# A convolution and attention kernel on one core: output stores issued before most of the loads of the image after next, and the orders inside attention written anew

## What is computed

```python
per_g = perception.reshape(b, M, 9 * C, h, w)              # 3x3 neighbourhood; M=32 groups of C=16
hdn = relu(einsum('bmchw,mdc->bmdhw', per_g, w1) + b1)     # 64 hidden channels a group
x1 = x + einsum('bmdhw,mcd->bmchw', hdn, w2) + b2
theta, phi, g = (projections of x1 from 512 to 128 channels)
attn = softmax(einsum('bno,bom->bnm', theta, phi), axis=-1)
y = einsum('bnm,bmo->bno', attn, g)
z = einsum('co,bno->bcn', w_w, y) + w_b                    # then batch norm with stored statistics
out = z + x1
```

## Time and profile before

| what | value |
|---|---|
| time, median of 3 runs (lowest to highest) | 1736.95 us (1734.25 to 1737.31) |
| the profiled execution, its own time | 1739.32 us |
| its span in the profile | 1737.5 us |
| mean granted TensorE clock | 0.962 of full speed |
| TensorE busy | 1551.6 us (89%) |
| VectorE, ScalarE, GpSimd busy | 875.1, 765.2 and 249.6 us |
| main memory traffic | 361.84 MB, 208 GB/s over the span; the DMA queue 64.2% busy |

### The profile page before, as it was taken

How to read it: one execution, slowest core, us unless ns; L and a number is a source line. 1 busy time by engine, 2 the same in 40 slices (tenths; PEclk the granted TensorE clock), 3 DMA queues, 4 the chain that set the end, 5 groups by cost and what they waited for, 6 DMA issues and landing times.

```text
span 1737.5 us, 23755 instructions
## 1 busy us (share of the span) xinstructions
PE 1551.6 (89%) x8324; PEld 838.4 (48%) x8324; DVE 875.1 (50%) x1200; ACT 765.2 (44%) x1205; POOL 249.6 (14%) x134
## 2 busy tenths in 40 slices
PE   5899898989989899898998989899898998989986
PEld 1265453645445364453645436354553654536455
DVE  0265363645627365373744627455273653737464
ACT  1444354444535454354443535454344543534442
POOL 0030020301103020020301203021030300203021
PEclk8899999999999999999999999999999999999998
DMA  9675766757576485765757566575765757656325
GB/s 284 156 240 186 242 216 190 245 185 245 180 232 232 152 272 175 242 229 151 260 192 246 187 218 227 175 259 179 250 230 148 257 187 238 216 183 233 124 92 175
DMA packets 179006, 361.84 MB, mean 208 GB/s; under 512 B 12336, under 2 KB 120880, under 8 KB 178992
## 3 DMA queue, kind: packets, MB, share of 16 engines
q1 hardware_dynamic: 178992, 361.66, 64.2%
HBM read 252.56 MB, written 109.05 MB: 208 GB/s over the span
## 4 chain that ended last, share of the span: by engine, by line
issue 85%; POOL 12%; DMA 1%; DVE 1%; PE 1%; POOLq 0%; ACT 0%; DVEq 0%; SPq 0%
POOL probs L885 12%; DMA rows_out<-probs 1%; DMA x_lo<-rows_out 1%; DVE x_lo L752 0%; PE ps L463 0%; PE ps L465 0%; PE ps L464 0%; DVE probs L743 0%; ACT x_hi L613 0%; POOLq L883 0%; DVE x L770 0%; POOLq L896 0%; DVE arena L758 0%; DVE neg_max L725 0%; ACT y_hi L623 0%
## 5 line engine op out<-in xcount | busy, mean ns | idle before, releaser
L397 PE MATMUL ps<-windows,w_main 128*64 128x512 f32 x2048 | 501.2, 616 | 51.9 <-ACT hidden L585 19.0
L885 POOL TENSOR_TENSOR probs<-probs,row_inv 128x1024 f32<-128x1024 f32 x128 | 248.9, 1950 | 1459.2 <-DVE row_inv L731 1459.2
L585 ACT ACTIVATE hidden<-ps,columns 128x512 f32<-128x512 f32 x512 | 315.4, 689 | 248.5 <-PE ps L408 228.6
L397 PEld LDWEIGHTS ps<-windows,w_main 128*64 128x64 f32 x2048 | 130.3, 138 | 375.8 <-issue 191.8
L417 PE MATMUL ps<-hidden,w2s 128*32 128x512 f32 x1024 | 148.9, 656 | 77.5 <-DVE x L706 77.5
L752 DVE TENSOR_TENSOR x_lo<-x_lo,x_hi 128x1024 fp32r<-128x1024 f32 x128 | 170.4, 1331 | 70.4 <-ACT x_hi L613 69.5
L713 DVE TENSOR_TENSOR x_lo<-x,x_hi 128x512 fp32r<-128x512 f32 x128 | 88.5, 691 | 221.8 <-ACT x_hi L593 219.9
L706 DVE SCALAR_TENSOR_TENSOR x<-ps,columns,windows 128x512 f32<-128x512 f32 x128 | 95.3, 744 | 200.4 <-DMA out<-x 104.6
L608 ACT ACTIVATE probs<-ps,neg_max 128x1024 f32<-128x1024 f32 x128 | 142.8, 1116 | 102.7 <-DVE neg_max L725 98.3
L613 ACT CAST x_hi<-x_lo 128x1024 fp32r<-128x1024 f32 x128 | 134.1, 1047 | 113.5 <-DMA x_lo<-rows_out 113.5
L725 DVE TENSOR_REDUCE neg_max<-ps 128x1 f32<-128x1024 f32 x128 | 155.2, 1213 | 53.6 <-PE ps L450 51.4
(11 more groups left out here) (55 smaller groups left out, 1541.8 us busy)
## 6 DMA issues: line engine op xcount, KB each, us to landing
windows<-in_x SPq DMA_DIRECT2D x208, 562.0 KB, 7.6
rows_out<-probs SPq DMA_DIRECT2D x128, 512.0 KB, 5.1
x_lo<-rows_out SPq DMA_DIRECT2D x128, 512.0 KB, 4.4
out<-x SPq DMA_DIRECT2D x64, 512.0 KB, 3.6
windows<-in_x SPq DMA_DIRECT2D x32, 421.5 KB, 7.1
windows<-in_x SPq DMA_DIRECT2D x32, 409.9 KB, 8.2
windows<-in_x SPq DMA_DIRECT2D x32, 281.0 KB, 9.3
rows_out<-hidden SPq DMA_DIRECT2D x16, 512.0 KB, 2.8
```

The source lines that it names most:

```text
L397: mm(ps[rows, hidden_bank(s, q), :], w_main[:, p, which, :], shifted(windows[:, w, :], unit // UNITS, half), start=True, stop=False, skip_ ...
L585: activation(hidden[:, q, :], ps[:, hidden_bank(s, q), :], ACT.Relu, bias=b1s[:, column:column + 1]).then_inc(hidden_ready, 1)
L885: nc.gpsimd.tensor_tensor(rows, rows, row_inv[:, e].to_broadcast([P, PIXELS]), ALU.mult).then_inc(normalized, 1)
```

## The change

No operation is added or taken away; only orders change, on SyncE, TensorE, ScalarE and VectorE. GpSimd's order stays. The core of the diff:

```diff
@@ SyncE, batch
-                    load_freed(n + 1, GROUPS - 1)
+                    load_freed(n + 1, 3)
+                send_g(n)
                 send_row(n, 0)
-                send_g(n)
+                fetch_g(n)
+                send_row(n, 1)
                 fetch_row(n, 0)
-                send_row(n, 1)
-                fetch_g(n)
+                send_row(n, 2)
                 fetch_row(n, 1)
...
                 store_quarter(n, 2)
                 if has_second:
                     load_freed(n + 2, 0)
-                    load_freed(n + 2, 1)
                 store_quarter(n, 3)
                 if has_second:
+                    load_freed(n + 2, 1)
                     load_freed(n + 2, 2)
@@ TensorE, batch
                 scores(n, 3)
+                if has_next:
+                    mains(n + 1, 0, range(0, 3))
                 scores(n, 4)
...
                 attend(n, 0, has_next)
-                if has_next:
+                scores(n, 7)
+                output(n, 0, 0)
+                if has_next:
+                    mains(n + 1, 1, range(1, 3))
                     dx(n + 1, 0)
-                    mains(n + 1, 1, range(1, 3))
-                outputs(n, 0)
-                scores(n, 7)
+                output(n, 0, 1)
...
-                    image_slot(n + 1, 4)
-                    mains(n + 1, 5, every)
+                    mains(n + 1, 4, range(0, 4))
+                attend(n, 3, has_next)
+                if has_next:
+                    dx(n + 1, 3)
+                    hidden_shared(n + 1, 4)
+                output(n, 3, 0)
+                output(n, 3, 1)
+                if has_next:
+                    mains(n + 1, 5, range(0, 4))
                     hidden_shared(n + 1, 5)
-                attend(n, 3, has_next)
-                if has_next:
                     dx(n + 1, 4)
-                outputs(n, 3)
-                if has_next:
-                    image_slot(n + 1, 6)
-                    image_slot(n + 1, 7)
+                    mains(n + 1, 6, range(0, 4))
+                    hidden_shared(n + 1, 6)
+                    dx(n + 1, 5)
+                    mains(n + 1, 7, range(0, 4))
+                    dx(n + 1, 6)
+                    hidden_shared(n + 1, 7)
@@ ScalarE, batch
                 exp_rows(n, 3)
+                round_g(n)
                 round_row(n, 0)
-                round_g(n)
                 exp_rows(n, 4)
                 if has_next:
-                    relus(n + 1, 0, range(0, 2))
+                    relus(n + 1, 0, range(0, 1))
                 round_row(n, 1)
                 if has_next:
-                    relus(n + 1, 0, range(2, 4))
+                    relus(n + 1, 0, range(1, 4))
+                round_row(n, 2)
                 exp_rows(n, 5)
...
+                    relus(n + 1, 5, range(0, 3))
+                    round_x1(n + 1, 4)
+                    relus(n + 1, 5, range(3, 4))
```

More of the change, by code:

```diff
@@ L499, in batch @@
             def batch(n, has_next):
-                every = range(GROUP_PAIRS)
                 project(n, 0, TH)
-                dx(n, SLOTS - 1)
+                dx(n, 7)
                 project(n, 0, PH)
@@ L511, in batch @@
                 scores(n, 3)
+                if has_next:
+                    mains(n + 1, 0, range(0, 3))
                 scores(n, 4)
                 if has_next:
-                    mains(n + 1, 0, every)
+                    mains(n + 1, 0, range(3, 4))
                     hidden_shared(n + 1, 0)
@@ L529, in batch @@
                     hidden_shared(n + 1, 1)
-                outputs(n, 1)
+                output(n, 1, 0)
+                output(n, 1, 1)
                 if has_next:
-                    mains(n + 1, 2, every)
+                    mains(n + 1, 2, range(0, 4))
+                    mains(n + 1, 3, range(0, 1))
                     hidden_shared(n + 1, 2)
@@ L629, in batch @@
             def batch(n, has_next):
-                every = range(GROUP_PAIRS)
                 bias_projection(n, 0, TH)
-                round_x1(n, SLOTS - 1)
+                round_x1(n, 7)
                 bias_projection(n, 0, PH)
@@ L656, in batch @@
                 round_y(n, 1)
+                if has_next:
+                    relus(n + 1, 1, range(0, 3))
                 round_row(n, 4)
                 if has_next:
-                    relus(n + 1, 1, every)
+                    relus(n + 1, 1, range(3, 4))
                 round_row(n, 5)
@@ L664, in batch @@
                     relus(n + 1, 2, range(0, 3))
+                    round_x1(n + 1, 1)
                 round_row(n, 6)
@@ L667, in batch @@
                     relus(n + 1, 2, range(3, 4))
[L668 to L669 removed]
                 round_row(n, 7)
                 if has_next:
[L672 removed]
+                    relus(n + 1, 3, range(0, 3))
+                if has_next:
                     round_x1(n + 1, 2)
[L674 to L675 removed]
+                    relus(n + 1, 3, range(3, 4))
                 round_y(n, 3)
                 if has_next:
[L678 to L680 removed]
+                    round_x1(n + 1, 3)
+                    relus(n + 1, 4, range(0, 4))
+                if has_next:
+                    relus(n + 1, 5, range(0, 3))
+                    round_x1(n + 1, 4)
+                    relus(n + 1, 5, range(3, 4))
+                    relus(n + 1, 6, range(0, 4))
+                    round_x1(n + 1, 5)
+                    relus(n + 1, 7, range(0, 4))
+                    round_x1(n + 1, 6)
             act.wait_ge(var_ready, 1)
@@ L778, in batch @@
             def batch(n, has_next):
[L779 removed]
+                sum_x1(n, 7)
+                split_x1(n, 7)
                 split_projection(n, 0, TH)
[L781 removed]
                 split_projection(n, 0, PH)
@@ L817, in batch @@
                 transpose_row(n, 6)
+                add_out(n, 1, 0)
+                add_out(n, 1, 1)
+                transpose_row(n, 7)
                 split_row(n, 4)
-                add_outs(n, 1)
                 split_row(n, 5)
-                transpose_row(n, 7)
                 if has_next:
@@ L838, in batch @@
                     split_x1(n + 1, 3)
-                split_y(n, 3)
-                add_outs(n, 3)
+                add_out(n, 3, 0)
+                add_out(n, 3, 1)
                 if has_next:
-                    for s in range(GROUPS, SLOTS - 1):
-                        sum_x1(n + 1, s)
-                        split_x1(n + 1, s)
+                    sum_x1(n + 1, 4)
+                    split_x1(n + 1, 4)
+                    sum_x1(n + 1, 5)
+                    split_x1(n + 1, 5)
+                    sum_x1(n + 1, 6)
+                    split_x1(n + 1, 6)
             steps = [0]
```

55 lines of the change are left out of this document (30 added, 25 removed).

## The result

The changed kernel takes 1636.83 us in the median of four runs (1630.14 to 1638.91) beside 1737.13 for the kernel before on the same chip: a ratio of 0.9416, interval 0.9386 to 0.9447. Forecast were 1627 and 1600 to 1668.

A forecast was written before the change was run, and what follows sets the result against it. TensorE was taken to wait mainly at `dx` of slot 5 for a store queued behind loads. -7.4 a round fourteen times (-104), -1 and -5 gave -110 from 1739.3: 1629, median 1627; 8-in-10 range 1600 to 1668.

The forecast's parts named there:

- The store and the stall: At `dx` of slot 5: store no longer behind g = 1 loads, stall gone (-5.45), lower clock gone (-2.3), per loaded round.
- The small waits: In attention outside its entrance: waits at `scores(4)`, at `mains` behind an exponential and at `attend(1)` go, -2.6 a round.
- The entrance without backlog: Where rows first come back in attention: waits of 1.6 at `mains` of slot 1, 1.7 at `attend(0)`; +2.0 a round.
- The backlog: In the DMA queue: window loads, g = 1 now begun later, delay the first send; +1.0 a round, bounds 0 and 2.5.
- rival 1: Clock falls at attention's entrance: 2.3 a round, 1680 with a backlog of 2.5, 1648 to 1660 either alone; shared chance 0.24.
- the signs named for a wrong forecast: Wait over 3 at `mains` of slot 1 or `attend(0)` with slower matmuls; first send landing 5+ after issue; unfound row wait.
- The fifteenth round and the last image: At the program's end: fifteenth round from 98.54 to 97.55, -1; last image's rows 6 and 7 sent earlier, -5.

The follow-up runs named there:

- window 18 whole: Changed kernel with window 18 fetched as two DMAs of all 128 partitions and half the columns each, not two of 64 partitions: 1598.87 us, ratio 0.9221.

## Why the prediction was right, point by point

**The store and the stall: right.** -5.45 and -2.3 came as forecast. The stall is 0, the store lands 3.2 to 3.5 after its issue in the loaded rounds but the first, where 2.9 and 7.8 had bounded it.

**The small waits: right.** No wait at `scores(4)`, `mains` behind the exponential or `attend(1)` is left in the fourteen rounds, apart from gaps of one missing record.

**The entrance without backlog: over-sized.** I had 1.6 and 1.7. The rounds without backlog show 1.1 and 1.0. In the eighth round `exp_rows(4)` starts 30.6 us after the start of the first projection, just as forecast, and `mains` of slot 1 at 32.4 in place of 32.6, with TensorE there 0.3 later than forecast. The second wait came out of the one half to one transfer taken for the queueing of row 1: its rounding starts 32.7 after the round's start, where 34.0 was forecast.

**The backlog: under-sized.** I took +1.0 with bounds 0 and 2.5. The send of g lands 2.3 later than an empty queue's 2.6 in the mean of rounds 2 to 15, and up to 5.4 later. In waits this is 1.4 a round (3.6 against 2.2 without a backlog), since a long wait at `mains` covers the one at `attend(0)`, and the clock comes on top. The term that was too small is the length of the stream: forecast were 11 for g = 1 and 22 for g = 2 and 3, measured are 12.9 and 22.8, so that it ends 23.5 after the round's start in place of 20.6. The 11 was what was left of a stretch of 14.4 less the store's 2.9, and the 22 was taken from one round. Slices at 3 us would have shown two speeds in that round (418 and 249 GB/s in the kernel before), and its other rounds that the end moves, from 13.2 to 16.2 after the second projection.

**The clock: half of rival 1.** It fell in nine of the fourteen rounds at the entrance, 1.3 us a round in the mean, where the forecast had none and the rival 2.3. The longest wait that left it alone was 3.17 us, and one of 2.12 did not (nor did one of 1.93 with window 18 whole), so the length of the wait alone doesn't decide. The Trainium skill's advice against idle gaps between bursts of matmuls (TensorE: Matmul & The Clock Gate, "Why this matters for your kernels") agrees for the long ones: the ninth round's 5.65 us had `mains` at 1.97 in place of 1.08.

The sum of a round: 92.9 + 3.6 of waits + 1.25 of clock = 97.75, against 93.25 + 3.3 + 1.0 = 97.55. Two of the signs named for a wrong forecast did come: waits over 3 us at `mains` with slower matmuls behind them, in seven of rounds 2 to 15, and sends of g that land 5 us or more after their issue, in six. The agreement of the mean to 0.2 us is partly luck: the entrance was too dear by 1.1 and the work by 0.35, and the backlog with its clock too cheap by 1.65.

**The fifteenth round and the last image: too hopeful.** 102.03 against 97.55 forecast: it starts with the worst backlog of all and has a wait of 6.27, which is not the rule: in the changed kernel's second execution that round waits 5.42, less than three others. From the start of the last stretch of the earlier trace rows to the end takes 75.02 where it took 76.56, so -1.5 and not -5: `attend(3)` comes 65.4 after the start where it came 65.7 after it, so row 7 is hardly earlier. Which instruction holds it there wasn't tried.

## What to carry to other kernels

When a store and loads share a queue, look at what stands ahead of the store at its issue, and whether what you move behind it has to be done before something else; here 5.45 + 2.3 us a round were gained at one end of the queue and 1.4 + 1.25 lost to the backlog at the other, until one window was moved as well. Cost a stream of loads by its slices and by the form of its transfers, not by a mean rate, and look at several rounds. And try the parts apart: the new engine orders alone lost 34 us, the new place of the store alone gained 52, and together they gained 100.

## What the runs showed of the hardware that was not expected

That the form of a load matters this much was not in the forecast: DMAs into all 128 partitions moved 403 to 418 GB/s in slices of 3 us, DMAs of 64 and 64 or 96 and 32 partitions 219 to 249 in the slices read that hold mostly them, with the DMA engines shown as fully busy in both; one such window of 562 KB held the queue for 3.6 us, in whole partitions for 1.5. The split ones are also the uneven ones: five whole windows took 6.84 to 6.89 us in round after round, one split window 2.7 to 4.5. The end of one and the same stream of window loads lay 16.9 to 22.7 us after the second projection in one execution of the changed kernel and 16.7 to 22.5 in another, and for the same round the two differed by up to 4.1.
